# A conditioned feed-forward kernel on one core: h0 rounded on GpSimd, the x sums of the last group from TensorE transposes and VectorE, first products reordered, projection weights stored row by row

## Chip, cores and metric

The kernel runs on one core of one Trainium2 chip. The metric is the device time of one execution in microseconds (us). In rows and text PE is TensorE (PEld its weight loads), DVE is VectorE, ACT is ScalarE, POOL is GpSimd, and SP is the engine that issues most of the transfers.

## What is computed

x has 32 batches of 64 rows with 512 columns, cond has 32 rows of 256. Only the parts that matter are kept:

```python
q_emb = relu(cond @ W3 + b3)
x_sum = sum(x, axis=1)                       # over the 64 rows of a batch
h0 = relu(((64 * x + x_sum) * q_emb[:, None, :]) @ W2 + b2)
w1, w2 = ternary(W_fc), ternary(W_proj)      # groups of 64 weights: q * mean(|w|), q in {-1, 0, 1}
h = square(relu(einsum('bsd,hd->bsh', h0, w1)))          # 2048 hidden columns
hn = h * rsqrt(mean(square(h)) + eps)
out = x + einsum('bsh,dh->bsd', hn, w2)
```

## The kernel before, in words

The 2048 rows of x are cut into four groups of 512 (`GROUPS`), each of eight batches. Activations stand turned: columns on the 128 partitions, the 512 rows of a group along the free axis. There are two stages.

**First stage, 16 units.** Unit u makes 128 columns of h0 for group u // 4: four fp32 products (`make_h0`, L292) from `x1_t`, the turned, summed and scaled x of the group. Ahead of it `sum_x(g)` (L276) multiplies the 16 blocks of `x_sb` (128 rows by 128 columns) by `sum_mat`, a matrix that turns a block and adds 64 * x and the sum of its batch in one fp32 product; `scale_x(g, k)` on DVE (L435) multiplies the result in `ps_out` by q. In PE's order `sum_x(1)`, `sum_x(2)` and `sum_x(3)` stand ahead of units 2, 6 and 10 (`SUMS_AT`). Every group's x goes through one buffer, `x_sb`. ACT adds the bias and takes the relu (`relu_h0`, L550), DVE rounds the result to fp32r (`round_h0`, L443) and POOL makes the rest (`rest_of_h0`, L602), so that two fast products replace a full one later.

**Beside it, the ternary weights.** The two weight matrices come in 16 pairs of row blocks (`PAIRS`). A pair is loaded by SP (`raw`), read twice by ACT (`read_pair`), summed by groups of 64 on DVE (`sum_pair`), spread by ACT (`spread_pair`), made ternary by three DVE instructions (`ternary_pair`), turned by a DMA transpose that SP issues (`turn_pair`, L219) and copied by ACT into `w_t` (`keep_pair`, L536). `STEP_AT_UNIT` says at which unit ACT and DVE do step i: on ACT it is keep i - 2, read i + 2 and spread i + 1; on DVE it is sum i + 1 and ternary i. There is one buffer `w_turned`: turn i waits until keep i - 1 is done. SP works in the order of its program: for each i it loads pair i + 4, then issues turn i; behind turn 1 it loads the x of group 2, behind turn 4 the x of group 3 (L256 to L259).

**Second stage, 64 tiles.** For each tile PE makes 128 hidden columns of a group (`hidden`, eight products, L308), ACT squares, DVE splits into `y_hi` and `y_lo` (`split_y`, L448), and PE projects (`project_tile`, eight products, L321) into the four banks of `ps_out`. POOL adds squares for the norm. Each projection product reads 512 columns of `w_t` as four runs of 128, each 512 columns from the next (L316). The stage's end of a group is `finish` (L482) and four stores.

**The start.** PE runs ten warm-up products of a constant (`WARM_UP`, L363), turns cond, runs two more, makes q (16 products, L375) and then the x sums of group 0, tile by tile (L377 to L385). All loads of the start are queued on SP and ACT in program order; the x of group 1 and the pairs from 2 on are queued behind the wait for the x sums of group 0 (L230).

Of the kernel before, what the change touches and what calls it, by code (L numbers as in the profile page):

```python
# [5 lines left out]
ALU = mybir.AluOpType  # L6
ACT = mybir.ActivationFunctionType
AX = mybir.AxisListType
# [16 lines left out]
QUAD = 32  # L25
WARM_UP = 10

# [6 lines left out]
def adaln_ffn(  # L34
# [44 lines left out]
    SUMS_AT = 2  # L79
    STEP_AT_UNIT = {0: 0, 1: 1, 3: 2, 4: 3, 5: 4, 7: 5, 8: 6, 9: 7, 11: 8, 12: 9, 13: 10, 15: 11}  # L80
    STEP_AT_TILE = {1: 12, 3: 13, 5: 14, 7: 15}
    KEEP_AT_TILE = {8: 14, 9: 15}

# [3 lines left out]
    with ExitStack() as ctx:  # L87
# [27 lines left out]
        w_tern = sb("w_tern", [P, RING, 2 * BANK], BF16)  # L115
        w_turned = sb("w_turned", [P, 2 * TT, P], BF16)
        abs_sum = sb("abs_sum", [P, SG], F32)
        scale = sb("scale", [P, RING, SG], BF16)
# [40 lines left out]
        q_ready = sem("q_ready")  # L159
        xt_done = sem("xt_done")  # L160
        x1_ready = sem("x1_ready")
        h0_done = sem("h0_done")
# [108 lines left out]
        def _(pe):  # L271
# [4 lines left out]
            def sum_x(g):  # L276
                pe.wait_ge(x_loaded, 16 * g)
                pe.wait_ge(x1_ready, KD * g)
                for k in range(KD):
                    for t in range(TT):  # L280
                        last = sum_x_block(t, k)
                    last.then_inc(xt_done, 1)
# [30 lines left out]
            def project_tile(v, t):  # L313
                g, j = v // HJ, v % HJ
                c, i = j // TT, j % TT
                w = w_t[:, HJ + KD * c:HJ + KD * (c + 1), i * P:(i + 1) * P]  # L316
                if j == 0:

                    wait(pe, finished, TT * (g - 1) + t + 1)
                for part in (y_hi, y_lo):  # L320
                    last = pe.matmul(ps_out[:, t, :], part[:, v % RING, t * P:(t + 1) * P], w,  # L321
                                     start=(j == 0 and part is y_hi), stop=(j == HJ - 1 and part is y_lo))
                if j == HJ - 1:
                    last.then_inc(tile_summed, 1)
                return last
# [43 lines left out]
            for i in range(2):  # L369
                pe.matmul(ps_acc[:, 1, 0:P], ident_f[:], ident_f[:], start=True, stop=True)  # L370
            pe.wait_ge(condt_ready, 1)
            pe.wait_ge(wq_loaded, 16)
            for m in range(KD):
                for k in range(KQ):
                    last = pe.matmul(ps_x[:, m * BATCHES:(m + 1) * BATCHES], wq_sb[:, k, m * P:(m + 1) * P],  # L375
                                     cond_t[:, k, :], start=(k == 0), stop=(k == KQ - 1))
            last.then_inc(q_done, 1)  # L377
            pe.wait_ge(consts_ready, 1)
            for t in range(TT):
                pe.wait_ge(x0_loaded[t], 16)  # L380
                for k in range(KD):
# [4 lines left out]
            for u in range(UNITS):  # L386
                if u % KD == SUMS_AT and u // KD + 1 < GROUPS:
                    sum_x(u // KD + 1)
                make_h0(u)
            for v in range(AHEAD):  # L390
# [14 lines left out]
        def _(dve):  # L405
# [29 lines left out]
            def scale_x(g, k):  # L435
                dve.wait_ge(xt_done, KD * g + k + 1)
                wait(dve, h0_done, KD * (g - 1))
                x1 = x1_t[:, g % RING, k, :].rearrange("p (b n) -> p b n", n=N)
                dve.tensor_tensor(x1, ps_out[:, k, :].rearrange("p (b n) -> p b n", n=N),  # L439
                                  q_t[:, k, g * GB:(g + 1) * GB].rearrange("p (b o) -> p b o", o=1).to_broadcast([P, GB, N]),  # L440
                                  ALU.mult).then_inc(x1_ready, 1)

            def round_h0(u):  # L443
                g, m = u // KD, u % KD
                dve.wait_ge(h0_relued, u + 1)
                dve.tensor_copy(h0_hi[:, m, g * BANK:(g + 1) * BANK], h0_f[:, u % RING, :]).then_inc(h0_hi_done, 1)  # L446

# [49 lines left out]
            for u in range(UNITS):  # L497
                g, m = u // KD, u % KD
                if u > 0:
                    round_h0(u - 1)  # L500
                if g + 1 < GROUPS and m == SUMS_AT:
                    for k in range(KD):
                        scale_x(g + 1, k)
                if u in STEP_AT_UNIT:
                    step(STEP_AT_UNIT[u])
            round_h0(UNITS - 1)
            for v in range(TILES):
# [14 lines left out]
        def _(act):  # L522
# [13 lines left out]
            def keep_pair(i):  # L536
                at = PAIRS[i][1]
                act.wait_ge(turned, 16 * (i + 1))
                act.activation(w_t[:, at:at + 2, :].rearrange("p i w -> p (i w)"),  # L539
                               w_turned[:].rearrange("p b w -> p (b w)"), ACT.Copy).then_inc(wt_ready, 1)  # L540

# [59 lines left out]
        def _(pool):  # L601
            def rest_of_h0(u):  # L602
                g, m = u // KD, u % KD
                cols = slice(g * BANK, (g + 1) * BANK)
                pool.wait_ge(h0_hi_done, u + 1)
                pool.tensor_tensor(h0_lo[:, m, cols], h0_f[:, u % RING, :], h0_hi[:, m, cols], ALU.subtract).then_inc(h0_split, 1)  # L606
# [14 lines left out]
            for u in range(UNITS):  # L621
                rest_of_h0(u)

# [34 lines left out]
```

## Time and profile before

| | |
|---|---|
| median of three runs | 323.41 us (322.25 to 323.43) |
| profiled execution, its time | 322.98 us |
| its span in the trace | 321.0 us |
| PE busy | 315.2 us (98% of the span) |
| DVE busy | 210.6 us (66%) |
| ACT busy | 192.3 us (60%) |
| POOL busy | 112.9 us (35%) |
| DMA | 27.02 MB, mean 84 GB/s |

The profiled execution is the program's own time of 322.98 us with a span of 321.0 us; 2 us lie around the span. Busy time of PE is modelled for pipelined products, so 98% says that it hardly waits, not that each product is as short as it could be.

### The profile page before, as it was taken

How to read it: one execution, taken by the hardware profiler on the slowest of the kernel's cores; microseconds unless marked ns; L12 is line 12 of the kernel's file. 1: busy time of each engine (PE TensorE's matmuls, PEld its weight loads, DVE VectorE, ACT ScalarE, POOL GpSimd, SP SyncE). 2: the span in 40 equal slices, each digit the busy share in tenths (PEclk: the TensorE clock that was granted, in tenths of full speed). 3: DMA queues.
4: the chain of work that ended last, by engine and by line, in shares of the span. 5: the costliest groups of instructions: out<-in, count | busy, mean ns of one | idle time of the engine just before them, and what ended most of it. 6: DMA issues, size and time to landing. Idle time of an engine off the chain costs nothing.

```text
span 321.0 us, 3855 instructions
## 1 busy us (share of the span) xinstructions
PE 315.2 (98%) x1336; PEld 239.8 (75%) x1336; DVE 210.6 (66%) x290; ACT 192.3 (60%) x282; POOL 112.9 (35%) x94
## 2 busy tenths in 40 slices
PE   8999999999999999999999999999999999999995
PEld 7764554644888788888888888888888888888884
DVE  0447989798998856577555565855565575665545
ACT  1639898799996876444555444554445554445550
POOL 1003333334553435414334441334443314443330
PEclk9999999999999999999999999999999999999999
DMA  6993959678731110007000000510000015000003
GB/s 190 300 315 84 267 157 255 172 146 263 130 52 34 33 36 1 0 0 263 0 0 2 0 0 0 198 68 0 2 0 0 0 64 199 0 0 2 0 1 132
DMA packets 31331, 27.02 MB, mean 84 GB/s; under 512 B 18736, under 2 KB 20816, under 8 KB 31312
## 3 DMA queue, kind: packets, MB, share of 16 engines
q1 hardware_dynamic: 29984, 26.25, 29.8%
q10 hardware_dynamic: 1328, 0.53, 0.6%
q8 instruction: 10, 0.16, 0.2%
q14 instruction: 9, 0.07, 0.1%
HBM read 18.39 MB, written 4.19 MB: 70 GB/s over the span
## 4 chain that ended last, share of the span: by engine, by line
PE 69%; ACT 10%; DVE 7%; issue 7%; DMA 5%; SPq 0%; POOL 0%; DVEq 0%; ACTq 0%; POOLq 0%
PE ps_out L321 34%; PE ps_acc L308 31%; DMA w_turned<-w_tern 3%; DVE abs_sum L412 3%; DMA raw<-in_L_ffn_W_proj_dram 3%; DVE x_t L439 2%; ACT w_scale L532 2%; ACT h_f L554 2%; PE ps_acc L363 1%; ACT x_t L562 1%; ACT w_abs L526 1%; ACT x_t L559 1%; PE ps_out L273 1%; ACT w_t L539 1%; ACT w_sign L527 1%
## 5 line engine op out<-in xcount | busy, mean ns | idle before, releaser
L210 POOL TENSOR_TENSOR wv_sb<-wv_sb 128x512 f32<-128x512 f32 x55 | 82.2, 1494 | 113.9 <-ACT wv_sb L565 113.9
L321 PE MATMUL ps_out<-w_t,y_hi 128*128 128x512 f32 x256 | 101.7, 397 | 0.2 <-DVE y_lo L454 0.2
L321 PE MATMUL ps_out<-w_t,y_lo 128*128 128x512 f32 x256 | 100.9, 394 | 0.0
L308 PE MATMUL ps_acc<-h_hi,w_t 128*128 128x512 f32 x256 | 100.1, 391 | 0.0
L308 PE MATMUL ps_acc<-h_lo,w_t 128*128 128x512 f32 x256 | 100.0, 391 | 0.0
L454 DVE TENSOR_TENSOR y_lo<-x_t,y_hi 128x512 fp32r<-128x512 f32 x64 | 91.3, 1427 | 2.2
L559 ACT ACTIVATE x_t<-ps_acc 128x512 f32<-128x512 f32 x64 | 38.1, 595 | 81.0 <-PE ps_acc L308 81.0
L452 DVE CAST y_hi<-x_t 128x512 fp32r<-128x512 f32 x64 | 29.5, 461 | 73.2 <-PE ps_out L321 65.7
L321 PEld LDWEIGHTS ps_out<-w_t,y_hi 128*128 128x128 f32 x256 | 48.1, 188 | 11.7 <-DVE y_lo L454 0.6
L321 PEld LDWEIGHTS ps_out<-w_t,y_lo 128*128 128x128 f32 x256 | 48.3, 189 | 10.9
L308 PEld LDWEIGHTS ps_acc<-h_hi,w_t 128*128 128x128 f32 x256 | 48.3, 189 | 10.6 <-issue 0.2
L292 PE MATMUL ps_acc<-x_t,wv_sb 128*128 128x512 f32 x128 | 55.8, 593 | 0.3 <-DVE x_t L439 0.3
L308 PEld LDWEIGHTS ps_acc<-h_lo,w_t 128*128 128x128 f32 x256 | 48.1, 188 | 10.5 <-issue 0.2
L292 PEld LDWEIGHTS ps_acc<-x_t,wv_sb 128*128 128x128 f32 x128 | 23.9, 190 | 29.3 <-issue 28.4
L606 POOL TENSOR_TENSOR h_lo<-h_f,h_hi 128x512 fp32r<-128x512 f32 x16 | 20.4, 1272 | 60.9 <-DVE h_hi L446 60.9
L565 ACT ACTIVATE wv_sb<-x_t 128x512 f32<-128x512 f32 x64 | 40.5, 632 | 2.0
L562 ACT ACTIVATE x_t<-x_t 128x512 f32<-128x512 f32 x64 | 40.4, 631 | 2.0
L526 ACT ACTIVATE w_abs<-raw 128x1024 bf16<-128x1024 f32 x16 | 16.7, 1047 | 6.2 <-DMA raw<-in_L_ffn_W_proj_dram 4.9
L532 ACT ACTIVATE w_scale<-scale 128x1024 bf16<-128x1024 bf16 x16 | 16.8, 1048 | 6.1 <-DVE scale L415 5.9
L539 ACT ACTIVATE w_t<-w_turned 128x1024 fp32r<-128x1024 bf16 x16 | 16.8, 1050 | 4.8 <-DMA w_turned<-w_tern 4.8
L412 DVE TENSOR_REDUCE abs_sum<-w_abs 128x16 f32<-128x1024 bf16 x16 | 19.4, 1212 | 0.1
L527 ACT ACTIVATE w_sign<-raw 128x1024 bf16<-128x1024 f32 x16 | 16.7, 1044 | 0.0
(48 smaller groups left out, 148.7 us busy)
## 6 DMA issues: line engine op xcount, KB each, us to landing
x_sb<-in_x_dram SPq DMA_DIRECT2D x7, 1024.0 KB, 6.3
raw<-in_L_ffn_W_fc_dram SPq DMA_DIRECT2D x8, 512.0 KB, 5.7
raw<-in_L_ffn_W_proj_dram SPq DMA_DIRECT2D x8, 512.0 KB, 6.1
out_dram<-x_t SPq DMA_DIRECT2D x16, 256.0 KB, 2.5
x_sb<-in_x_dram SPq DMA_DIRECT2D x4, 256.0 KB, 5.6
wv_sb<-in_L_cond_W_dram SPq DMA_DIRECT2D x4, 256.0 KB, 7.2
x_t<-in_L_cond_W_dram ACTq DMA_DIRECT2D x1, 512.0 KB, 4.9
w_turned<-w_tern SPq DMA_TRANSPOSE x16, 3.1
```

The source lines that it names most:

```text
L210: engine.tensor_tensor(sq_acc[:], sq_acc[:], y_sq[:, v % SQ_RING, :], ALU.add).then_inc(sq_added, 1)
L292: last = pe.matmul(ps_acc[:, u % ACC_RING, :], wv_sb[:, k, m * P:(m + 1) * P], x1_t[:, g % RING, k, :], start=(k == 0), stop=(k == KD - 1))
L308: last = pe.matmul(ps_acc[:, (UNITS + v) % ACC_RING, :], w_t[:, j, k * P:(k + 1) * P], part[:, k, g * BANK:(g + 1) * BANK], start=(k == 0 ...
L321: last = pe.matmul(ps_out[:, t, :], part[:, v % RING, t * P:(t + 1) * P], w, start=(j == 0 and part is y_hi), stop=(j == HJ - 1 and part i ...
L412: dve.tensor_reduce(abs_sum[:], grouped(w_abs[:, i % READ_RING, :]), AX.X, ALU.add).then_inc(sum_ready, 1)
L452: dve.tensor_copy(y_hi[:, v % RING, :], y[:, v % RING, :]).then_inc(hi_done, 1)
L454: dve.tensor_tensor(y_lo[:, v % RING, :], y[:, v % RING, :], y_hi[:, v % RING, :], ALU.subtract).then_inc(split, 1)
L532: act.activation(w_scale[:, i % RING, :].rearrange("p (s w) -> p s w", w=TERN_GROUP), scale[:, i % RING, :].rearrange("p (s o) -> p s o", ...
L559: act.activation(relu_y[:, v % RING, :], ps_acc[:, (UNITS + v) % ACC_RING, :], ACT.Relu).then_inc(relued, 1)
L562: act.activation(y[:, v % RING, :], relu_y[:, v % RING, :], ACT.Square).then_inc(y_ready, 1)
L565: act.activation(y_sq[:, v % SQ_RING, :], y[:, v % RING, :], ACT.Square).then_inc(sq_ready, 1)
L606: pool.tensor_tensor(h0_lo[:, m, cols], h0_f[:, u % RING, :], h0_hi[:, m, cols], ALU.subtract).then_inc(h0_split, 1)
```

## The change

The rounding of h0 goes from DVE to POOL, where one function now rounds and makes the rest. Group 3's x is turned by 16 PE transposes ahead of unit 8 (not by 16 products ahead of unit 10), and DVE adds up the batches: for each k a reduction, a multiply-add and the multiplication by q, one k at each of the units 8 to 11. In the start five warm-up products go, and the q products move behind the second of the four x tiles. Steps 5, 6 and 10 of the weights move by one unit: to 6, 7 and 14, from 7, 8 and 13. The projection weights are stored by ACT so that one product reads 512 neighbouring columns. SP's program is as it was.

```diff
-WARM_UP = 10
+WARM_UP = 5
...
-    STEP_AT_UNIT = {0: 0, 1: 1, 3: 2, 4: 3, 5: 4, 7: 5, 8: 6, 9: 7, 11: 8, 12: 9, 13: 10, 15: 11}
+    STEP_AT_UNIT = {0: 0, 1: 1, 3: 2, 4: 3, 5: 4, 6: 5, 7: 6, 9: 7, 11: 8, 12: 9, 14: 10, 15: 11}
+    def sums_by_vector(g):
+        return g == GROUPS - 1
...
@@ PE
                     for t in range(TT):
-                        last = sum_x_block(t, k)
+                        if sums_by_vector(g):
+                            last = pe.transpose(ps_out[:, k, t * P:(t + 1) * P], x_sb[:, t, k * P:(k + 1) * P], ident_f[:])
+                        else:
+                            last = sum_x_block(t, k)
                     last.then_inc(xt_done, 1)
...
-                c, i = j // TT, j % TT
-                w = w_t[:, HJ + KD * c:HJ + KD * (c + 1), i * P:(i + 1) * P]
+                w = w_t[:, HJ + j, :]
...
-            pe.wait_ge(condt_ready, 1)
-            pe.wait_ge(wq_loaded, 16)
-            for m in range(KD):
-                for k in range(KQ):
-                    last = pe.matmul(ps_x[:, m * BATCHES:(m + 1) * BATCHES], wq_sb[:, k, m * P:(m + 1) * P],
-                                     cond_t[:, k, :], start=(k == 0), stop=(k == KQ - 1))
-            last.then_inc(q_done, 1)
             pe.wait_ge(consts_ready, 1)
             for t in range(TT):
+                if t == TT // 2:
+                    pe.wait_ge(condt_ready, 1)
+                    pe.wait_ge(wq_loaded, 16)
+                    for m in range(KD):
+                        for k in range(KQ):
+                            last = pe.matmul(ps_x[:, m * BATCHES:(m + 1) * BATCHES], wq_sb[:, k, m * P:(m + 1) * P],
+                                             cond_t[:, k, :], start=(k == 0), stop=(k == KQ - 1))
+                    last.then_inc(q_done, 1)
                 pe.wait_ge(x0_loaded[t], 16)
...
-                if u % KD == SUMS_AT and u // KD + 1 < GROUPS:
+                if u % KD == SUMS_AT and u // KD + 1 < GROUPS - 1:
                     sum_x(u // KD + 1)
+                if u == KD * (GROUPS - 2):
+                    sum_x(GROUPS - 1)
                 make_h0(u)
@@ DVE
-                dve.tensor_tensor(x1, ps_out[:, k, :].rearrange("p (b n) -> p b n", n=N),
+                src = ps_out[:, k, :].rearrange("p (b n) -> p b n", n=N)
+                if sums_by_vector(g):
+                    at = 2 * k
+                    wait(dve, summed, at)
+                    dve.tensor_reduce(batch_sum[:], src, AX.X, ALU.add).then_inc(summed, 1)
+                    dve.wait_ge(summed, at + 1)
+                    dve.scalar_tensor_tensor(out=x1, in0=src, scalar=float(N),
+                                             in1=batch_sum[:].rearrange("p (b o) -> p b o", o=1).to_broadcast([P, GB, N]),
+                                             op0=ALU.mult, op1=ALU.add).then_inc(summed, 1)
+                    dve.wait_ge(summed, at + 2)
+                    src = x1
+                dve.tensor_tensor(x1, src,
...
-            def round_h0(u):
-                g, m = u // KD, u % KD
-                dve.wait_ge(h0_relued, u + 1)
-                dve.tensor_copy(h0_hi[:, m, g * BANK:(g + 1) * BANK], h0_f[:, u % RING, :]).then_inc(h0_hi_done, 1)
...
-                if u > 0:
-                    round_h0(u - 1)
-                if g + 1 < GROUPS and m == SUMS_AT:
+                if g + 1 < GROUPS - 1 and m == SUMS_AT:
                     for k in range(KD):
                         scale_x(g + 1, k)
+                if g == GROUPS - 2:
+                    scale_x(g + 1, m)
                 if u in STEP_AT_UNIT:
                     step(STEP_AT_UNIT[u])
-            round_h0(UNITS - 1)
@@ ACT, keep_pair
-                act.activation(w_t[:, at:at + 2, :].rearrange("p i w -> p (i w)"),
-                               w_turned[:].rearrange("p b w -> p (b w)"), ACT.Copy).then_inc(wt_ready, 1)
+                if at < HJ:
+                    act.activation(w_t[:, at:at + 2, :].rearrange("p i w -> p (i w)"),
+                                   w_turned[:].rearrange("p b w -> p (b w)"), ACT.Copy).then_inc(wt_ready, 1)
+                else:
+
+                    c, first = (at - HJ) // KD, (at - HJ) % KD * P
+                    act.activation(w_t[:, HJ + TT * c:HJ + TT * (c + 1), first:first + 2 * P].rearrange("p j (i w) -> p i j w", i=2),
+                                   w_turned[:].rearrange("p (i j) w -> p i j w", i=2), ACT.Copy).then_inc(wt_ready, 1)
@@ POOL
-            def rest_of_h0(u):
+            def split_h0(u):
                 g, m = u // KD, u % KD
                 cols = slice(g * BANK, (g + 1) * BANK)
+                pool.wait_ge(h0_relued, u + 1)
+                pool.tensor_copy(h0_hi[:, m, cols], h0_f[:, u % RING, :]).then_inc(h0_hi_done, 1)
                 pool.wait_ge(h0_hi_done, u + 1)
                 pool.tensor_tensor(h0_lo[:, m, cols], h0_f[:, u % RING, :], h0_hi[:, m, cols], ALU.subtract).then_inc(h0_split, 1)
```

## Rows read from the trace of the kernel before

**Rows 1.** The page: busy time by engine, and the chain's shares by engine.
```profile
PE 315.2 (98%) x1336; PEld 239.8 (75%) x1336; DVE 210.6 (66%) x290; ACT 192.3 (60%) x282; POOL 112.9 (35%) x94
...
PE 69%; ACT 10%; DVE 7%; issue 7%; DMA 5%; SPq 0%; POOL 0%; DVEq 0%; ACTq 0%; POOLq 0%
```

**Rows 2.** The waits of PE: who waited, for whom, us, times, longest.
```profile
PE ps_acc L292 <- DVE x_t L439: 0.3, 1, 0.3
PE ps_out L273 <- DMA x_sb<-in_x_dram: 0.2, 1, 0.2
```

**Rows 3.** PE in order of time: start us, us, line, products, [idle before].
```profile
1.52 4.64 PE L363 MATMUL ps_acc<-ident_f 128*128 128x128 f32 x20 [1.52 <-POOL ident_f L610]
...
9.14 3.82 PE L273 MATMUL ps_out<-sum_mat,x_sb 128*128 128x128 f32 x32
13.24 7.10 PE L292 MATMUL ps_acc<-x_t,wv_sb 128*128 128x512 f32 x16 [0.28 <-DVE x_t L439]
...
37.97 2.27 PE L273 MATMUL ps_out<-sum_mat,x_sb 128*128 128x128 f32 x18 [0.20 <-DMA x_sb<-in_x_dram]
...
41.65 13.90 PE L292 MATMUL ps_acc<-x_t,wv_sb 128*128 128x512 f32 x32
55.38 3.73 PE L273 MATMUL ps_out<-sum_mat,x_sb 128*128 128x128 f32 x32
```

**Rows 4.** Groups by line and shape on PE: count | busy us, mean ns.
```profile
L273 PEld LDWEIGHTS ps_out<-sum_mat,x_sb 128*128 128x128 f32 x128 | 14.8, 192 | 2.0 <-DMA x_sb<-in_x_dram 1.0 <-issue 1.0
...
L363 PEld LDWEIGHTS ps_acc<-ident_f 128*128 128x128 f32 x20 | 4.3, 331 | 1.5 <-POOL ident_f L610 1.5
...
L366 PE MATMUL ps_acc<-ident_f,h_f 32*128 32x32 f32 x2 | 0.4, 300 | 0.0
```

**Rows 5.** The chain that ended last, second stage: start us, us, line.
```profile
144.83 1.86 PE ps_out L321 x8
146.69 1.82 PE ps_acc L308 x8
```

**Rows 6.** SP in order of time: DMA issues of the first stage.
```profile
30.82 1.24 SPq L222 DMA_TRANSPOSE w_turned<-w_tern  x1
32.10 0.58 SPq L231 DMA_DIRECT2D x_sb<-in_x_dram  x1
...
47.05 1.24 SPq L222 DMA_TRANSPOSE w_turned<-w_tern  x1
48.33 0.59 SPq L231 DMA_DIRECT2D x_sb<-in_x_dram  x1
```

**Rows 7.** The tile x_sb, the one load issued at 48.3 us, and its landing.
```profile
L231 SPq DMA_DIRECT2D x_sb<-in_x_dram x1: 589/589/589, 48.3 to 48.3; - x1
...
DMA to landing us min/median/max: 6.3/6.3/6.3
```

**Rows 8.** ACT in order of time, first stage: start us, us, line, [idle before].
```profile
22.17 1.06 ACT L526 ACTIVATE w_abs<-raw 128x1024 bf16<-128x1024 f32 x1 [4.87 <-DMA raw<-in_L_ffn_W_proj_dram]
...
29.68 1.06 ACT L539 ACTIVATE w_t<-w_turned 128x1024 fp32r<-128x1024 bf16 x1
...
34.05 1.05 ACT L532 ACTIVATE w_scale<-scale 128x1024 bf16<-128x1024 bf16 x1 [1.43 <-DVE scale L415]
...
35.59 1.04 ACT L539 ACTIVATE w_t<-w_turned 128x1024 fp32r<-128x1024 bf16 x1
...
40.82 1.06 ACT L539 ACTIVATE w_t<-w_turned 128x1024 fp32r<-128x1024 bf16 x1 [0.78 <-DMA w_turned<-w_tern]
...
45.92 1.06 ACT L539 ACTIVATE w_t<-w_turned 128x1024 fp32r<-128x1024 bf16 x1
```

**Rows 9.** Groups by line and shape on DVE and POOL: count | busy us, mean ns.
```profile
L606 POOL TENSOR_TENSOR h_lo<-h_f,h_hi 128x512 fp32r<-128x512 f32 x16 | 20.4, 1272 | 60.9 <-DVE h_hi L446 60.9
...
L488 DVE SCALAR_TENSOR_TENSOR x_t<-ps_out,rstd,x_sb 128x512 f32<-128x512 f32 x16 | 11.0, 744 | 0.3
...
L446 DVE CAST h_hi<-h_f 128x512 fp32r<-128x512 f32 x16 | 7.8, 490 | 10.6 <-ACT h_f L554 10.4
```

More of the change, by code:

```diff
@@ L116, in adaln_ffn @@
         w_turned = sb("w_turned", [P, 2 * TT, P], BF16)
+        batch_sum = sb("batch_sum", [P, GB], F32)
         abs_sum = sb("abs_sum", [P, SG], F32)
@@ L160, in adaln_ffn @@
         xt_done = sem("xt_done")
+        summed = sem("summed")
         x1_ready = sem("x1_ready")
@@ L621, in _ @@
             for u in range(UNITS):
-                rest_of_h0(u)
+                split_h0(u)
             pool.wait_ge(h0_split, UNITS)
```

## The prediction

> **What bounds the kernel now.** I read the page first: PE is busy 98% of the span, DVE 66%, ACT 60% and POOL 35% [rows 1]. The chain gives 69% to PE and the rest to ACT, DVE and transfers, all of it in the first stage; a chain can run through other engines while PE is busy beside it, so the next view is what PE itself waited for. That is almost nothing: 0.3 us for the first scaled x and 0.2 us for the x of group 2 [rows 2]. The order of time says the same: each stretch of products begins where the one before ends [rows 3]. So PE sets the time from 1.5 us to the last projection. Taking work from DVE gives nothing by itself; only fewer or shorter products on PE gain, and any wait that PE is given counts in full.
>
> **The loads that PE meets with no slack.** The x of group 2 is issued at 32.10 us and PE waits for it until 37.97 [rows 3, 6]. The x of group 3 is issued at 48.33 and lands 6.3 us later, at 54.6 [rows 6, 7]; PE asks for it at 55.38 [rows 3]. The slack is 0.8 us. This load stands on SP behind turn 4, turn 4 waits for keep 3 on ACT, and so back, turn by turn, to turn 1, because there is one turned buffer.
>
> **The change part by part.** The base is the profiled execution, 322.98 us (321.0 of span and 2 around it), 0.4 us under the median of the runs.
>
> *Start.* Ten warm-up products take 4.64 us [rows 3], so five fewer are 5 x 0.46 = 2.3 us. But PE is slow at first: one record there takes 4.64 / 20 = 0.23 us, and 3.82 / 32 = 0.12 us in the x sums of group 0 from 9.14 us [rows 3]. The first x tile's eight records now fall into the slow part and cost 8 x 0.11 = 0.9 us more. Net -1.4 us; bounds -2.3 and 0 (the x tiles or weights may land later than PE now asks). The q products only change places; their result is needed after the last x sum as before. The gain goes on to SP, whose later loads stand behind the x sums of group 0, and with these to ACT, which waited 4.87 us for pair 2 [rows 8].
>
> *Group 3's x at unit 8 and not at unit 10.* This is the step that decides. PE comes to the place ahead of unit 8 by 16 sums and two units after the x of group 2 has landed: 41.65 - 37.97 = 3.7 us, and, as four units take 55.38 - 41.65 = 13.7 us [rows 3], 6.9 us more; 10.5 us in all. The x of group 3 landed 54.6 - 38.0 = 16.7 us after that of group 2. With SP's order unchanged, PE would wait 6.2 us. What do the moved steps give back? The distance is three cycles of turn and keep, 47.05 - 30.82 = 16.2 us [rows 6], by keeps 5.9, 5.2 and 5.1 us [rows 8]. In the first, ACT waited 1.43 us for DVE's scale [rows 8]; DVE no longer waits for the relu of each unit, so that goes: 4.4. In the second, turn 2 is then issued 1.5 us closer behind the x of group 2, which shares its queue, and ACT was already waiting 0.78 us for it; part of the gain comes back there: 5.9, between 5.2 and 6.7. The third is step 5, a unit earlier, but the keep follows the landing of turn 3, not the unit: 5.1. Sum 15.4, and 0.5 for the longer landing; the wait is 15.4 + 0.5 - 10.5 = **5.4 us**. The lower bound is ACT without any wait, three times its own 4.4 us: from the spread at 34.05 to the keep at 35.59 a copy and a relu take 1.54 us [rows 8], and a cycle has three copies more of some 0.95. That is 13.2, a wait of 3.2 us. The upper one is 17.0, a wait of 7.0. Units 8 to 11 need only group 2, but stand behind the transposes in PE's order, so nothing covers it.
>
> *The transposes themselves.* A sum block has two records, 16 blocks 3.73 us [rows 3]. The two transposes of cond have one record each [rows 4], so I take half: 3.73 - 1.87 = 1.9 us less; bounds -2.8 (a record half as long) and 0 (two passes after all).
>
> *Projection from neighbouring columns.* Eight projection products take 1.86 us in the chain, eight hidden products 1.82 [rows 5], with equal size and type; the hidden ones read one run of 512, the projections four of 128. If the runs make the difference, 64 x 0.04 = -2.6 us; bounds -3.2 (rounding of both rows) and 0 (something else makes it, such as the change between four banks).
>
> The Trainium skill speaks against this part: its page "Advanced Engine Details and Errata", section "SBUF Cachelines", says that accesses that stay within one 16-byte line run at full speed. Runs of 128 floats stay within lines as well as one run of 512 does, but for three jumps. By that rule the projections stay at 1.86 us, and the sum below is 2.6 us higher; no row here has the two layouts in one kind of product, so the rule is a rival.
>
> *Rounding on POOL.* DVE loses 16 x 0.49 = 7.8 us [rows 9] and gets four reductions and four multiply-adds, no more than 0.75 us each by the nearest row, 6.0 us; it has slack for both. One k takes about 2.2 us, a unit 3.4, and unit 12 comes 13.7 us after the transposes, so the scaled x is in time. On POOL the rounding costs between 0.49 (DVE's) and 1.27 us (POOL's own subtraction) [rows 9]; with the subtraction 1.8 to 2.5 us a unit, under PE's 3.4. It shows only at the end of the stage, where steps 10 and 11 now follow each other on ACT and the last relu and POOL's last work come later: +0.3, between 0 and 1.0. The copies of the projection weights by ACT keep their element count, so I cost them at nothing; were one longer, it would lie in the same chain of turns, of which PE needs the projection pairs only in the second stage.
>
> *The clock after the wait.* In the start, after PE had done nothing, weight loads took 331 ns; the same shape took 192 ns later [rows 4]. I read this as the lower of the two levels (1.2 and 2.4 GHz). It lasted at least the 4.6 us of the warm-up and at most 7.6 us, to the x sums at full speed [rows 3]; half of it is lost, 2.3 to 3.8 us, and I take 2.9. No row shows PE idle for more than 0.3 us later, so whether 5 us bring the lower level back has no row; bounds 0 and 3.8. I take 2.9, because the only idle time before work in this trace was followed by slow work.
>
> The Trainium skill's page "TensorE: Matmul & The Clock Gate", section "Part 4: PE-mode transpose", adds that transposes don't engage the full clock as products do. By that rule the 16 transposes don't help the clock up again, and the lower level lasts as much longer as they take. No run here shows it yet.
>
> **The sum.** 322.98 - 1.4 + 5.4 - 1.9 - 2.6 + 0.3 + 2.9 = **325.7 us**.
>
> **The rivals.** *The clock holds.* All else as above: 322.8 us. For it: only 5 us are idle. Against it: the start. *The runs of 128 cost nothing* (the first rule above): 328.3 us with the fall of the clock, 325.4 without. For it: all else in the two kinds of product differs too (banks, weights). Against it: both kinds have the same size and type. *The clock stays low over the transposes* (the second rule): 16 records at 0.23 us, then as long a slow stretch as in the start; 16 x 0.11 = 1.8 us more, 327.5 us. *The wait is short*, the case on the other side: the turns land at once, and ACT's own 4.4 us set each cycle. Then PE waits 3.2 us and the clock has less reason to fall: 322.98 - 1.4 + 3.2 - 1.9 - 2.6 + 0.3 = 320.6 us, and less with a shorter landing. It decides from about 4 us of wait downward. For it: ACT waited only in two of the three cycles shown, 1.43 and 0.78 us [rows 8]. Against it: turn 2 comes closer behind a megabyte in its own queue.
>
> **How the numbers follow.** Forecast 0.40, clock holds 0.24, runs cost nothing 0.10, clock low over the transposes 0.08, short wait 0.18. The measurement of this kernel can tell about 0.5%, 1.6 us, from no change: faster is under 321.8, slower over 325.0. Faster is the short wait, nearly all of it, and a small part of the held clock: 0.20. Within 0.5% is most of the held clock and the lower part of the forecast: 0.28. Slower is the rest, 0.52. The range goes from the short wait with a quick landing, 320.0, to the costless runs with a lower clock, 328.5. For the forecast alone the wait's bounds give 323.5 to 327.3.
>
> **What would show it.** Right: PE idle some 5 us ahead of 16 transposes, ended by the load of x; that load issued about 14 us or more after the load of group 2; weight loads over 300 ns behind it; the chain with eight projections in 1.82 us. Wrong: no wait of PE ahead of unit 8, or one under 3 us; products at full speed right behind the wait; 1.86 us for eight projections; a wait of PE for POOL's rounding at the first hidden tiles, which I have at under 1 us. A load that lands early, or a start that gains nothing, would move the sum by up to 2 us without changing the story.

## The result and the profile after

The changed kernel takes **328.72 us** (median of four runs, 328.39 to 329.26) against 323.42 us for the kernel before in the same comparison: a ratio of 1.018, with a 95% interval of 1.0154 to 1.0199. It is slower by 5.3 us. The forecast was slower by 2.3 us, and the time lies 0.2 us above the range. The profiled execution has a span of 326.8 us, 5.8 us over the one before; the working below goes by that pair. All times below are of fast executions: one execution of the kernel with the wait filled ran at a granted clock of 0.56 throughout, took 538.08 us and is left out of its median.

The page of the kernel after: busy time by engine, and the chain's shares by engine. They answer [rows 1].

```profile
PE 316.4 (97%) x1310; PEld 238.2 (73%) x1310; DVE 218.8 (67%) x282; ACT 191.6 (59%) x282; POOL 126.7 (39%) x110
...
PE 75%; ACT 9%; issue 5%; DMA 4%; DVE 4%; POOL 1%; SPq 1%; ACTq 0%; POOLq 0%; DVEq 0%
```

PE has 26 records less (1336 to 1310) and is still busy 1.2 us longer. So the loss can't all be waiting. Its waits in the kernel after, as [rows 2]:

```profile
PE ps_out L287 <- DMA x_sb<-in_x_dram: 4.7, 1, 4.7
PE ps_out L328 <- DVE y_lo L470: 0.3, 1, 0.3
```

One wait of 4.7 us is new. PE in order of time in the kernel after, answering [rows 3]; L287 is the transposes, L300 the units, L316 the hidden products, L328 the projection:

```profile
1.53 2.50 PE L370 MATMUL ps_acc<-ident_f 128*128 128x128 f32 x10 [1.53 <-POOL ident_f L633]
...
5.32 3.09 PE L278 MATMUL ps_out<-sum_mat,x_sb 128*128 128x128 f32 x16
...
12.27 7.10 PE L300 MATMUL ps_acc<-x_t,wv_sb 128*128 128x512 f32 x16 [0.28 <-DVE x_t L460]
...
36.52 3.73 PE L278 MATMUL ps_out<-sum_mat,x_sb 128*128 128x128 f32 x32
...
51.83 3.48 PE L287 MATMUL ps_out<-ident_f,x_sb 128*128 128x128 f32 x16 [4.71 <-DMA x_sb<-in_x_dram]
...
82.37 0.80 PE L316 MATMUL ps_acc<-h_hi,w_t 128*128 128x512 f32 x1
...
88.70 0.47 PE L328 MATMUL ps_out<-w_t,y_hi 128*128 128x512 f32 x1 [0.29 <-DVE y_lo L470]
```

The same two starts in the kernel before:

```profile
79.15 0.79 PE L308 MATMUL ps_acc<-h_hi,w_t 128*128 128x512 f32 x1
...
85.05 0.39 PE L321 MATMUL ps_out<-w_t,y_hi 128*128 128x512 f32 x1
```

So the first stage ends 3.2 us later, and by the first projection it is 3.65 us. The other 2.15 us of the 5.8 come after that, in the rest of the second stage, for which the list of waits has none. The chain that ended last, in the second stage (start us, us, line), beside [rows 5]:

```profile
152.68 1.86 PE ps_out L328 x8
154.55 1.85 PE ps_acc L316 x8
```

Eight projection products still take 1.86 us, and eight hidden products have gone from 1.82 to 1.85. Where a figure with three decimals stands below, it is the mean, from start to start, of such groups of eight over some 50 tiles between 115 and 300 us of the order of time: before 1.820 hidden and 1.865 projection, after 1.857 and 1.868. 64 tiles times 0.037 us are 2.4 us, about the missing 2.15. Nothing in the prediction touched the hidden products, so this was the first thing to find.

### The profile page after: what moved, and what is told of

The parts are those of the page before. It is cut to its first block, busy times and chain, and to the rows that moved or that the text cites. A ratio compares the mean times of both kernels' runs of the same rounds, so it can differ in the third digit from the quotient of the medians.

```text
span 326.8 us, 3811 instructions
## 1 busy us (share of the span) xinstructions
PE 316.4 (97%) x1310; PEld 238.2 (73%) x1310; DVE 218.8 (67%) x282; ACT 191.6 (59%) x282; POOL 126.7 (39%) x110
## 4 chain that ended last, share of the span: by engine, by line
PE 75%; ACT 9%; issue 5%; DMA 4%; DVE 4%; POOL 1%; SPq 1%; ACTq 0%; POOLq 0%; DVEq 0%
PE ps_out L328 33%; PE ps_acc L316 31%; PE ps_acc L300 6%; DMA raw<-in_L_ffn_W_proj_dram 2%; DMA x_sb<-in_x_dram 2%; ACT w_scale L547 2%; PE ps_out L278 1%; ACT x_t L583 1%; ACT w_abs L541 1%; ACT w_sign L542 1%; ACT x_t L580 1%; DVE abs_sum L422 1%; PE ps_out L287 1%; ACT h_f L575 1%; PE ps_acc L370 1%
## 5 line engine op out<-in xcount | busy, mean ns | idle before, releaser
L328 PE MATMUL ps_out<-w_t,y_hi 128*128 128x512 f32 x256 | 101.8, 398 | 0.4 <-DVE y_lo L470 0.3
L316 PE MATMUL ps_acc<-h_hi,w_t 128*128 128x512 f32 x256 | 101.2, 395 | 0.0
L328 PE MATMUL ps_out<-w_t,y_lo 128*128 128x512 f32 x256 | 100.8, 394 | 0.0
L316 PE MATMUL ps_acc<-h_lo,w_t 128*128 128x512 f32 x256 | 100.6, 393 | 0.0
L328 PEld LDWEIGHTS ps_out<-w_t,y_hi 128*128 128x128 f32 x256 | 48.1, 188 | 12.6 <-issue 0.7
L316 PEld LDWEIGHTS ps_acc<-h_hi,w_t 128*128 128x128 f32 x256 | 48.1, 188 | 11.7 <-issue 0.2
L328 PEld LDWEIGHTS ps_out<-w_t,y_lo 128*128 128x128 f32 x256 | 48.1, 188 | 11.4
L300 PE MATMUL ps_acc<-x_t,wv_sb 128*128 128x512 f32 x128 | 55.9, 594 | 0.3 <-DVE x_t L460 0.3
L316 PEld LDWEIGHTS ps_acc<-h_lo,w_t 128*128 128x128 f32 x256 | 48.0, 188 | 11.1 <-issue 0.2
L300 PEld LDWEIGHTS ps_acc<-x_t,wv_sb 128*128 128x128 f32 x128 | 24.2, 192 | 29.2 <-issue 28.7
L627 POOL CAST h_hi<-h_f 128x512 fp32r<-128x512 f32 x16 | 11.4, 710 | 49.7 <-ACT h_f L575 49.7
L629 POOL TENSOR_TENSOR h_lo<-h_f,h_hi 128x512 fp32r<-128x512 f32 x16 | 22.8, 1424 | 1.3
```

The costliest lines, as they stand in the source:

```text
L300: last = pe.matmul(ps_acc[:, u % ACC_RING, :], wv_sb[:, k, m * P:(m + 1) * P], x1_t[:, g % RING, k, :], start=(k == 0), stop=(k == KD - 1))
L316: last = pe.matmul(ps_acc[:, (UNITS + v) % ACC_RING, :], w_t[:, j, k * P:(k + 1) * P], part[:, k, g * BANK:(g + 1) * BANK], start=(k == 0 ...
```

## The experiments

Times are medians; "before" is the kernel before, run beside the version. My theory behind the result was that the lost time had three sources: the wait, the clock behind it, and something in the second stage that is not the row layout. The rivals for the last were the rows (the new projection operand slowing its neighbours) and the place of the tiles. The change declares a new tile of 32 bytes a partition, `batch_sum`, ahead of `abs_sum`, and every tile behind it in memory, `y_hi` and `y_lo` among them, lies 32 bytes further on.

### The rows, the place, and POOL

**The rows alone**, in the kernel before (with the matching `keep_pair` of the change):

```diff
-                c, i = j // TT, j % TT
-                w = w_t[:, HJ + KD * c:HJ + KD * (c + 1), i * P:(i + 1) * P]
+                w = w_t[:, HJ + j, :]
```

> The kernel before with the projection rows alone made contiguous (ACT's copy and PE's operand). In the changed kernel eight projections still take 1.86 us and eight hidden products went from 1.82 to 1.85 us, 64 x 0.03 = 2 us. Theory A, the layout of the rows does this to the hidden products: hidden 1.85, projections 1.86, about 325.5 us. Theory B, the new tile of 32 bytes that stands ahead of y_hi and y_lo in memory does it, and the rows gain nothing: 1.82 and 1.86, 323.4 us. Theory C, my forecast holds for the rows and something else took the gain back: projections 1.82, 320.8 us.

Measured: 322.46 us against 322.62, ratio 0.999 (0.9976 to 1.0003). The chain of the second stage:

```profile
152.90 1.82 PE ps_acc L308 x8
154.72 1.86 PE ps_out L320 x8
```

Neighbouring columns leave the projection at 1.86 us (mean 1.870) and the hidden products at 1.82 (mean 1.815). Each mean differs by 0.005 us from the kernel before, in opposite directions; their sum is 3.685 us in both kernels. So the rows change nothing.

**The new tile alone**, unused, in the kernel before:

```diff
+        batch_sum = sb("batch_sum", [P, GB], F32)
         abs_sum = sb("abs_sum", [P, SG], F32)
```

> The kernel before with a tile of 32 bytes a partition put ahead of abs_sum, scale, y_hi and y_lo, which nothing uses. Theory A (rows): no change, 323.4 us, hidden 1.82 us for eight. Theory B (addresses): hidden 1.85 us, about 325.5 us.

Measured: 325.59 us against 322.62, ratio 1.0081 (1.0057 to 1.0106). No instruction differs; the program only has other addresses. Its chain:

```profile
151.30 1.85 PE ps_acc L309 x8
153.16 1.86 PE ps_out L322 x8
```

This is the chain of the changed kernel. Hidden mean 1.858, so 64 x 0.038 = 2.4 us, against 3.0 in the medians.

**The change with the old rows** (the row edit undone in both places):

> The changed kernel with the old layout of the projection rows. Theory A (rows): hidden back at 1.82 us for eight, about 326.6 us (328.7 - 2). Theory B (addresses): hidden stays at 1.85 us, 328.7 us. Theory C (rows gain, something else costs): slower than the changed kernel, about 331 us.

Measured: 327.8 us against 322.62, ratio 1.0161 (1.0124 to 1.0198), hidden 1.849, projection 1.874. Its interval overlaps that of the change, as the run of the rows alone says it should.

**The change with its tile last**, behind the other tiles of that memory:

```diff
-        batch_sum = sb("batch_sum", [P, GB], F32)
         abs_sum = sb("abs_sum", [P, SG], F32)
...
         rstd = sb("rstd", [P, TT], F32)
+        batch_sum = sb("batch_sum", [P, GB], F32)
```

> The changed kernel with its new tile batch_sum (32 bytes a partition) declared behind the last tile, so that y_hi and y_lo stand where they stood before. Theory B (addresses): eight hidden products back from 1.85 to 1.82 us, 64 x 0.035 = 2.2 us: about 326.5 us; the wait for x and the slow transposes stay. If the address of y_hi and y_lo is not it: 328.7 us.

Measured: 326.42 us against 322.54, ratio 1.0114 (1.0087 to 1.0141), hidden back at 1.820. One line in another place of the list gives back about 2 us: 2.3 us between the medians of the two versions, and the intervals of their ratios don't meet.

**POOL's rounding alone**, in the kernel before:

```diff
-                if u > 0:
-                    round_h0(u - 1)
...
+                pool.wait_ge(h0_relued, u + 1)
+                pool.tensor_copy(h0_hi[:, m, cols], h0_f[:, u % RING, :]).then_inc(h0_hi_done, 1)
```

> The kernel before with h0 rounded by POOL and not by DVE, nothing else changed. By the forecast it is free, 0 to +1 us: 323.4 to 324.4 us, all of it at the first projection. Theory D, that the rounded values or the longer use of POOL slow the hidden products of the second stage: hidden 1.85 us for eight, about 325.5 us.

Measured: 322.42 us against 322.62, ratio 0.9991 (0.9975 to 1.0007). POOL rounds in 719 ns in the mean, and nobody on PE waits for it.

### Which tile's place, and how

**y_hi and y_lo alone, 32 bytes on.** A tile of 16 bytes (`mean_sq`, which takes 32) is declared ahead of them instead of behind, so that of all other tiles only `mean_sq` itself changes its place:

```diff
+        mean_sq = sb("mean_sq", [P, TT], F32)
         y_hi = sb("y_hi", [P, RING, BANK], F32R)
         y_lo = sb("y_lo", [P, RING, BANK], F32R)
...
-        mean_sq = sb("mean_sq", [P, TT], F32)
```

> The kernel before with mean_sq (16 bytes a partition) declared ahead of y_hi, so that y_hi and y_lo alone move by 32 bytes; abs_sum and scale stay. If it is the place of y_hi and y_lo, which DVE writes while PE runs the hidden products: hidden 1.85 us for eight, about 325 us. If it is that of abs_sum or scale: 1.82 us and 322.6 us.

**64 bytes on** (`root` as well), and **96** (`rstd` too):

> The kernel before with mean_sq and root declared ahead of y_hi: y_hi and y_lo move by 64 bytes. If what counts repeats every 64 bytes, this is as before: hidden 1.82 us for eight, 322.6 us. If the old place is one good one among more distances: 1.85 us, about 325 us.

> The kernel before with mean_sq, root and rstd declared ahead of y_hi: y_hi and y_lo move by 96 bytes. 64 gave 1.84 for eight projections and 1.83 for eight hidden products, 32 gave 1.86 and 1.86, the old place 1.86 and 1.82. If the effect repeats every 64 bytes, this is like 32: 1.86 and 1.86, 325 us. If every place has its own value: something between, 322 to 324 us.

**y_lo alone, 32 bytes on** (a 32-byte tile between `y_hi` and `y_lo`):

> The kernel before with a free tile of 32 bytes between y_hi and y_lo: y_lo alone moves by 32 bytes. DVE writes y_hi in 0.43 us and y_lo in 1.67 us of the 1.82 us in which PE runs eight hidden products. If DVE's access to the moved tile slows the products read meanwhile: most of the 2.3 us of the move of both comes from y_lo alone, 324.5 us and 1.85 us for eight hidden products. If PE's own loads of the weights y_hi and y_lo are what counts, the projections change, and by half: 323.7 us.

| y_hi, y_lo moved by | us | before | ratio (95%) | eight hidden | eight projections |
|---|---|---|---|---|---|
| 0 | | | | 1.820 | 1.865 |
| 32, 32 | 324.97 | 322.54 | 1.0068 (1.0042 to 1.0093) | 1.860 | 1.865 |
| 64, 64 | 322.02 | 322.54 | 0.9985 (0.9968 to 1.0003) | 1.832 | 1.840 |
| 96, 96 | 323.0 | 322.81 | 1.0006 (0.9985 to 1.0027) | 1.822 | 1.863 |
| 0, 32 | 324.19 | 322.81 | 1.0041 (1.0017 to 1.0065) | 1.840 | 1.871 |

The chains of the second stage, moved by 32, then by 64, by 96, and y_lo alone:

```profile
150.82 1.85 PE ps_acc L308 x8
152.68 1.86 PE ps_out L321 x8
```

```profile
151.09 1.83 PE ps_acc L308 x8
152.93 1.83 PE ps_out L321 x8
```

```profile
150.99 1.86 PE ps_out L321 x8
152.85 1.82 PE ps_acc L308 x8
```

```profile
150.45 1.84 PE ps_acc L309 x8
152.29 1.87 PE ps_out L322 x8
```

Moving these two tiles is enough for the effect; the place of `mean_sq` is not it, because it stands in the same new place in the run with 96 bytes, which is as fast as before. The effect doesn't simply repeat every 64 bytes: by the sum of both means, 0 and 96 give 3.685 us, 32 gives 3.725 and 64 gives 3.672. y_lo by itself makes more than half of it (3.711 us). The sums are steady enough for this: in the nine traces read with both tiles at the old place, whatever else was changed, they lie between 3.685 and 3.687 us, and in the four traces with both tiles 32 bytes on, the changed kernel among them, between 3.723 and 3.725. The times of 64 and 96 can't be told from no change.

The odd thing is that the hidden products read `h0` and `w_t`, not `y_hi` or `y_lo`; those are being written by DVE meanwhile. DVE in the kernel with the unused tile, steady state:

```profile
155.13 0.43 DVE L453 CAST y_hi<-x_t 128x512 fp32r<-128x512 f32 x1 [1.60 <-PE ps_out L322]
155.59 1.66 DVE L455 TENSOR_TENSOR y_lo<-x_t,y_hi 128x512 fp32r<-128x512 f32 x1
```

Both instructions begin while PE runs eight hidden products (154.86 to 156.72 us); y_lo goes on for 0.5 us into the projections. That makes a collision of DVE's traffic with PE's reading plausible, but the same kernel speaks against it elsewhere. Its second and third hidden tiles, ahead of the first projection, with DVE splitting the first tile beside them:

```profile
82.72 0.39 PE L309 MATMUL ps_acc<-h_lo,w_t 128*128 128x512 f32 x1
...
85.44 0.40 PE L309 MATMUL ps_acc<-h_lo,w_t 128*128 128x512 f32 x1
```

```profile
83.52 1.15 DVE L453 CAST y_hi<-x_t 128x512 fp32r<-128x512 f32 x1 [0.50 <-ACT x_t L563]
84.71 0.69 DVE L455 TENSOR_TENSOR y_lo<-x_t,y_hi 128x512 fp32r<-128x512 f32 x1
```

Twelve products there take 2.72 us, 0.227 each, and so do the same twelve of the kernel before (82.10 to 84.82): there DVE's writing at the moved place does not slow them. POOL's squares and projections between the hidden products are missing in that stretch, and y_lo takes 0.69 us there and not 1.66; which of these differences counts was not tried. The Trainium skill's page "SBUF — State Buffer", section "SBUF: two separate sides", says that PE never waits on the other engines for SBUF; the measured change of the hidden products by a mere move of tiles is not explained by that, and no run here ties it to a port. **The place is shown as the cause; the mechanism stays open.**

### The wait and the clock

The wait, seen from SP (the kernel after; turn 1, the load of group 2's x, turns 2 to 4, the load of group 3's x):

```profile
28.68 1.24 SPq L227 DMA_TRANSPOSE w_turned<-w_tern  x1
29.96 0.58 SPq L236 DMA_DIRECT2D x_sb<-in_x_dram  x1
...
33.70 1.24 SPq L227 DMA_TRANSPOSE w_turned<-w_tern  x1
...
39.39 1.24 SPq L227 DMA_TRANSPOSE w_turned<-w_tern  x1
...
43.75 1.24 SPq L227 DMA_TRANSPOSE w_turned<-w_tern  x1
45.03 0.58 SPq L236 DMA_DIRECT2D x_sb<-in_x_dram  x1
```

The two loads stand 15.1 us apart (15.4 predicted), and the second lands 6.8 us after its issue. PE, which comes to the place at 47.1 us, waits until 51.83. Then the clock. The kernel after by stretches: us, PE busy (count), the same for PEld, DVE, ACT, POOL, then the granted clock, DMA share and GB/s:

```profile
46.00:50.00 4.00, 1.12 (x3) 0.19 (x1) 3.90 (x6) 4.00 (x6) 1.88 (x2) 1.00 0.97 235
50.00:52.00 2.00, 0.17 (x2) 0.18 (x3) 1.15 (x2) 1.45 (x2) 0.49 (x1) 1.00 1.40 373
52.00:54.00 2.00, 2.00 (x11) 2.00 (x11) 1.19 (x2) 0.00 (x0) 1.38 (x2) 0.52 0.97 199
54.00:56.00 2.00, 2.00 (x9) 1.62 (x8) 1.93 (x4) 0.00 (x0) 0.00 (x0) 0.63 0.49 175
56.00:58.00 2.00, 2.00 (x6) 0.88 (x5) 1.97 (x3) 0.00 (x0) 0.00 (x0) 1.00 0.00 0
```

The clock was 1.00 when PE stopped, and the column still gives 1.00 while PE waits. In the first two us of work behind the wait it is 0.52, close to the lower level of 1.2 GHz, which is 0.50; then 0.63, then 1.00 again. The loss by these rows is 2 x 0.48 + 2 x 0.37 = 1.7 us, that is 3.4 us at the lower level.

**The wait filled.** In the change with its tile last PE waits a little less, 4.1 us, and the clock falls as well:

```profile
51.09 3.03 PE L287 MATMUL ps_out<-ident_f,x_sb 128*128 128x128 f32 x16 [4.09 <-DMA x_sb<-in_x_dram]
```

In that kernel, 20 products of a constant, whose result nobody reads, ahead of the transposes:

```diff
                 if u == KD * (GROUPS - 2):
+                    for i in range(FILL):
+                        pe.matmul(ps_x[:, P:2 * P], ident_f[:], ident_f[:], start=True, stop=True)
                     sum_x(GROUPS - 1)
```

> The changed kernel with batch_sum declared last (326.4 us), and 20 constant products of 128 columns on PE right ahead of the transposes; they have no use and fill the 4.1 us of the wait for x. Theory: the idle time brings the lower clock back; then, without idle time, the granted clock stays at 1.00, the 16 transposes take 1.8 to 2.0 us instead of 3.0, the units behind them run at full speed, and the time is about 1.5 us less, 324.9 us, though PE waits for x as long as before. Rival: transposes are slow by themselves or don't keep the clock up: no change, 326.4 us.

> The kernel of wait_filled once more, for its trace. If the idle time brought the lower clock back: granted clock 1.00 from 46 us on, 16 transposes in 1.8 to 2.0 us and the 64 records of the units behind them in 27.4 us; with the wait, where the clock was low, they took 3.0 and 28.3 us.

Measured: 324.53 us against 322.92, ratio 1.0049 (1.0025 to 1.0074), and again 324.39 against 322.81, ratio 1.0049 (1.0023 to 1.0074). That is 1.9 to 2.0 us under the kernel without the filling (326.42), and the intervals of the ratios don't meet. The two are one kernel; the second has the trace shown: its filling and transposes, and a stretch by the columns above.

```profile
46.83 4.63 PE L400 MATMUL ps_x<-ident_f 128*128 128x128 f32 x40
51.30 1.91 PE L288 MATMUL ps_out<-ident_f,x_sb 128*128 128x128 f32 x16
...
52.00:54.00 2.00, 2.00 (x15) 1.52 (x13) 1.93 (x3) 0.00 (x0) 1.59 (x2) 1.00 0.84 94
```

The data come no earlier (51.30), but 16 transposes now take 1.91 us instead of 3.03, and the clock is 1.00. From the transposes to the first hidden product it takes 28.8 us (80.11 - 51.30); without filling, in the kernel with its tile last, 30.6 (81.65 - 51.09). So useless work in a wait that can't be avoided is worth 1.8 us here, and the fall of the clock is a cost of its own beside the wait.

**The wait removed at its source**: the load of group 3's x behind turn 3, in the change with its tile last.

```diff
-                if i == 4:
+                if i == 3:
                     load_x(3)
```

> The same, and SP loads the x of group 3 behind turn 3 and not behind turn 4, one cycle of 4.4 us earlier. If the wait of 4.7 us ahead of unit 8 is that load's place in SP's queue, it goes almost whole, and with it the slow transposes (some 1.5 us): 326.5 - 4.7 - 1.5 = about 320.3 us, under the kernel before. If only the wait goes and the slow transposes are their own price: 321.8 us. If the load is limited by what is queued with it and not by its place: no change, 326.5 us.

Measured: 322.05 us against 322.54, ratio 0.9981 (0.9964 to 0.9999), 4.4 us under the kernel with the load behind turn 4. Its transposes and PE's waits:

```profile
46.52 1.97 PE L287 MATMUL ps_out<-ident_f,x_sb 128*128 128x128 f32 x16
...
PE ps_out L328 <- DVE y_lo L470: 1.2, 2, 1.0
PE ps_acc L316 <- ACT h_f L575: 1.0, 1, 1.0
```

No wait and no slow clock: 16 transposes in 1.97 us, and the first hidden product at 75.39, 3.8 us ahead of the kernel before. But 2 us are given back: PE waits 1.0 us for the last relu and 1.0 us for the first `y_lo`. ACT shows why (first and last of a row of work that leaves no gap):

```profile
76.10 1.06 ACT L555 ACTIVATE w_t<-w_turned 128x1024 fp32r<-128x1024 bf16 x1
...
79.89 0.68 ACT L575 ACTIVATE h_f<-ps_acc,bv_t 128x512 f32<-128x512 f32 x1
```

Steps 10 and 11 of the weights stand on ACT ahead of the last relu. When PE gets there 3.8 us earlier, ACT is what is late.

**The group-3 move undone**, all else as in the change with its tile last (products at unit 10, `scale_x` as before):

```diff
     def sums_by_vector(g):
-        return g == GROUPS - 1
+        return False
...
-                if u % KD == SUMS_AT and u // KD + 1 < GROUPS - 1:
+                if u % KD == SUMS_AT and u // KD + 1 < GROUPS:
                     sum_x(u // KD + 1)
-                if u == KD * (GROUPS - 2):
-                    sum_x(GROUPS - 1)
```

> The changed kernel with batch_sum declared last and group 3's x summed in the old way, by 16 products ahead of unit 10, and scaled by DVE at unit 10; the start, POOL's rounding, the rows and the moved steps stay. Theory: the place ahead of unit 8 costs a wait of 4.1 us and a slow clock of 1.5 us, against 1.8 us that the transposes save: 326.4 - 4.1 - 1.5 + 1.8 = 322.6 us, up to 323.5 if the last relus come late. If the rest of the change is what costs: 326 us or more.

Measured: 322.0 us against 322.92, ratio 0.9951 (0.9931 to 0.997). There is no wait at unit 10, where the sums begin:

```profile
54.48 3.73 PE L278 MATMUL ps_out<-sum_mat,x_sb 128*128 128x128 f32 x32
```

Against its own before the move costs 3.9 + 0.9 = 4.8 us: the one part of the change that is meant for group 3 makes all of the loss that the tile's place doesn't make, and hides 0.9 us that the rest of the change gains.

### The start, and a version that beats both

**The start alone**, in the kernel before (five warm-up products less, q products behind the second x tile):

> The kernel before with the shorter start alone (five warm-up products, the q products behind the second x tile). In the changed kernel the first h0 product began 1.0 us earlier, 12.27 and not 13.24 us. If that goes through to the end, as PE sets the time: 321.5 us. If the x of group 2 or the weights take it back: 322.5 us.

Measured: 321.33 us against 322.92, ratio 0.9942 (0.992 to 0.9964); the span is 1.5 us shorter, and 1.5 us show at the first hidden product already (79.15 before):

```profile
77.65 0.79 PE L308 MATMUL ps_acc<-h_hi,w_t 128*128 128x512 f32 x1
```

**The early load with step 11 late.** As ACT was late behind the early load, step 11 goes into the second stage:

```diff
-    STEP_AT_UNIT = {... 14: 10, 15: 11}
-    STEP_AT_TILE = {1: 12, 3: 13, 5: 14, 7: 15}
+    STEP_AT_UNIT = {... 14: 10}
+    STEP_AT_TILE = {1: 11, 3: 12, 5: 13, 7: 14, 9: 15}
...
-    KEEP_AT_TILE = {8: 14, 9: 15}
+    KEEP_AT_TILE = {10: 14, 11: 15}
```

> The kernel of early_x_sum_last (322.05 us) with the last weight step of the first stage moved into the second: steps 11 to 15 at tiles 1, 3, 5, 7 and 9, the last two copies at tiles 10 and 11. In that kernel PE waited 1.0 us for the last relu of h0, which stood behind steps 10 and 11 on ACT, and 1.0 us for the first y_lo. If those two steps are the cause, both waits go: about 320 us, under the kernel before. If ACT and DVE then fall behind in the tiles: 321 to 322 us.

Measured: 320.68 us against 322.92, ratio 0.9927 (0.9902 to 0.9952). The wait for the last relu is gone, and this is what is left at the handover:

```profile
PE ps_out L328 <- DVE y_lo L470: 0.4, 1, 0.4
```

**The same with y_hi and y_lo 64 bytes on:**

> The kernel of early_x_step11_late (320.68 us) with y_hi and y_lo moved by 64 bytes. If the rates of y_shift_64 hold here, a tile of eight and eight products takes 3.67 and not 3.685 us: 64 x 0.015 = 1 us less, 319.7 us. If the sum of both only looked different: 320.7 us.

Measured: 319.46 us against 322.81, ratio 0.9891 (0.9851 to 0.993), hidden 1.832 and projection 1.839 (sum 3.671 against 3.685 in the kernel before). It is the fastest version, 1.1% under the kernel before and about 9 us under the change as it was made. That it beats the one above it is not shown: their intervals overlap, and the traced execution of this one waited for x again. Behind this wait of 1.36 us the transposes take the time of the full clock:

```profile
47.96 1.97 PE L287 MATMUL ps_out<-ident_f,x_sb 128*128 128x128 f32 x16 [1.36 <-DMA x_sb<-in_x_dram]
```

## Why the prediction was right and where it failed

The direction and the mechanism of the first stage held: the move of the transposes runs PE into a load that stands too late in SP's queue, and the clock falls behind that wait. The step that failed is the one for the second stage: the gain of 2.6 us from the projection rows measured 0, and the hidden products, which had no term, lost 2.2 us by the place of two tiles. The sum came out 3.1 us too low (+2.7 of the base predicted, +5.8 in the span). By its own terms:

| term | predicted us | measured us |
|---|---|---|
| start | -1.4 | -1.6 |
| wait for group 3's x | +5.4 | +4.7 |
| transposes | -1.9 | -1.8 |
| clock behind the wait | +2.9 | +1.7 |
| projection rows | -2.6 | 0 |
| handover, POOL | +0.3 | +0.4 |
| hidden products, by the place of y_hi and y_lo | none | +2.2 |
| sum | +2.7 | +5.6 (the span: +5.8) |

These two errors are 4.8 us together. The miss is smaller only because the wait and the clock came out 1.9 us cheaper than the sum had them; that is luck. So is the nearness of the rival of the costless rows, 328.3 us: it has no term for the place of the tiles, and the same 1.9 us stand against it. The range was also put together too narrowly: its upper end of 328.5 us is the rival of the costless rows with the forecast's own wait and clock (328.3), and the upper bounds that the prediction gave for these two, 7.0 and 3.8 us, were left out of it.

*Start.* The size was right, and partly by luck. Two x tiles, not one, fell into the slow part (16 records in 3.09 us), so the first h0 product came only 1.0 us earlier. The rest came at the x sums of group 2, where PE had waited before and no longer did: the units behind them start 1.6 us earlier (40.09 and 41.65). The start alone gave 1.5 us in the trace.

*Wait.* Right in mechanism: the issue distance of 15.1 us against 15.4, built from three turn-and-keep cycles, is the term that carried it. Its parts were off, and cancelled: the turns stand 5.0, 5.7 and 4.4 us apart, where the prediction had 4.4, 5.9 and 5.1. The wait by the same sum is 15.1 + 0.2 - 10.6 = 4.7 us. The 0.2, which the prediction had at 0.5, is the landing of 6.8 us less the 6.56 us between the issue of group 2's x and PE's start on it (36.52 - 29.96; 5.87 before). The rival of the short wait is out: only the third cycle has ACT's own 4.4 us.

*Transposes.* From the transposes to the first hidden product takes 28.9 us where PE did not wait (75.39 - 46.52), against 30.6 for the same work with sums before (79.15 - 48.5, where 48.5 is 41.65 and two units): 1.8 us, within its bounds. Single records in TensorE transposes was the right reading of the two transposes of cond.

*Clock.* It fell, as forecast; the rival that it holds is out. The term was mis-sized: I took half of the length of the slow start, 2.9 us; the slow stretch here was 3.4 us and cost 1.7. The argument from the start is weaker than it looked, because the column of the granted clock gives 1.00 for the first 12 us of both kernels; what speaks for it is that a transpose takes 3.48 / 16 = 0.22 us behind the wait, near the 0.23 us of a record in the start. The weight loads of the transposes took 226 ns and not over 300, so that sign of being right did not show. The rival with the clock low over the transposes, and as long a slow stretch as in the start behind them, is out in that form: the transposes end at about 55.1 us, and from 56 us on the clock is 1.00. Whether other products in their place would have brought it back sooner, no run separates.

*Projection rows.* This step failed, and by the most. It took a correlation between two rows of the chain, 1.86 and 1.82 us with different layouts, for a cause. One run of the layout alone shows 0 (a ratio of 0.999, and 3.685 us for eight and eight products in both kernels). The rival by the Trainium skill, "Advanced Engine Details and Errata", section "SBUF Cachelines", was right where I weighed it at 0.10: here runs of 128 floats go as fast as a run of 512 (1.865 and 1.870 us for eight projections). What does move these two numbers is in the table of places above: with y_hi and y_lo 64 bytes on, the projection takes 1.84 and the hidden products 1.83, with the old rows. The 0.04 us of difference on which the term stood belongs to one such place.

*What was not in the sum.* The new 32-byte tile, of which the prediction says nothing; I had read its declaration only as a buffer. It moves y_hi and y_lo, and this alone costs 2.4 us (the two tiles moved by 32 bytes) to 3.0 us (the new tile unused). The line that declares it ahead of `abs_sum` is part of the change, and the cut diff ahead of the prediction doesn't show it; a trace of the kernel before shows nothing that would have priced it.

*Handover.* The first `y_lo` came 0.3 us late and the step to the first projection grew by 0.4 us, as said. But a term that is small behind a wait of 4.7 us is not small without it: once the wait went, PE stood 2 us at the end of the stage, behind ACT's steps.

## What to carry to other kernels

Two rows of one profile that differ in several things don't price any one of them; a run with the one thing changed does. Before moving a consumer forward, look at how its load stands in the issuing queue, and move the load with it: here one index in the queue was worth 4.4 us, and filling the wait, where it can't be avoided, 1.9 us, because PE ran 3.4 us at the lower clock behind it. Treat a new tile, however small, as an edit of the memory map: declare it behind the tiles that the long loop uses, or compare the loop's rate before and after.

## What the runs showed of the hardware

The rate of TensorE products depended on the byte place of tiles that those products don't read: eight hidden products of 512 columns took from 1.820 to 1.860 us by moves of y_hi and y_lo of 32 to 96 bytes, up to 1% of the kernel's time; eight projections, which do read the two tiles, took from 1.840 to 1.871. After 4.7 us of idleness the granted clock, 1.00 before, was 0.52 in the first 2 us of work and 1.00 again some 4 us on; with the wait filled it stayed at 1.00. And TensorE transposes of 128 x 128 in fp32 run 16 in 1.97 us at the full clock, 0.12 us each, about half of an fp32 product of the same size (16 sums in 3.73 us).
